# Attention tail split in two and the gate kept in another buffer, in a fused attention and channel-mix layer

## The reference

```python
x = x + LN(attention(LN(x)))      # 16 heads of 64, rope over the whole width, banded softmax
x = x + LN(channel_mix(LN(x)))

# attention: blocks of 512 queries see their own block and the one before, inside a band
q, k, v = h @ Wq.T + bq, h @ Wk.T + bk, h @ Wv.T + bv       # q, k then rope
scores = einsum('qd,kd->qk', q, k) / 8;  band = (j >= i) & (j <= i + 512)
out = softmax(where(band, scores, min)) @ v;  return out @ Wo.T + bo

# channel mix, x_prev is x shifted by one token
xr, xk = mu_r*x + (1-mu_r)*x_prev, mu_k*x + (1-mu_k)*x_prev
r = sigmoid(xr @ W_r.T)
return r * (square(relu(xk @ W_k.T)) @ W_v.T)
```

## Time and profile before

| | |
|---|---|
| Median of 2 runs | 6762.48 us (6732.92 and 6792.04) |
| The profiled execution | 6755.53 us, of which the span of the slowest core (core 3) is 6754.0 us |
| Spans of the 8 cores | 6704.8 to 6754.0 us |
| Busy: PE, DVE, ACT, POOL | 3167.8, 3086.4, 1531.8, 874.3 us |
| Mean busy share of the 16 DMA engines by queue | 9.1%, 6.1%, 2.9% and less |
| Chain that ended last, by engine | PE 34%, DVE 33%, ACT 9%, issue 7%, DMA 7%, SPq 5% |

### The profile page before, as it was taken

How to read it: one execution, slowest core, us unless ns; L and a number is a source line. 1 busy time by engine, 2 the same in 40 slices (tenths; PEclk the granted TensorE clock), 3 DMA queues, 4 the chain that set the end, 5 groups by cost and what they waited for, 6 DMA issues and landing times.

```text
span 6754.0 us, 51815 instructions; the slowest of 8 cores (6704.8 to 6754.0 us)
## 1 busy us (share of the span) xinstructions
PE 3167.8 (47%) x11840; PEld 1243.5 (18%) x11840; DVE 3086.4 (46%) x4185; ACT 1531.8 (23%) x2881; POOL 874.3 (13%) x644
## 2 busy tenths in 40 slices
PE   0435526355254545545454364553645365363654
PEld 0112212122121212212121121221211122121221
DVE  2454344444454445344455444544445543444434
ACT  0111403214021220412203041130411114132141
POOL 0011211111111110211101011120111101111021
PEclk9857566575667657566575666656667575665756
DMA  6313020120201212012120301203012120211201
GB/s 198 95 38 87 4 98 24 38 87 4 97 25 59 66 38 87 1 59 66 34 91 19 94 13 50 75 19 94 13 50 75 38 87 1 93 32 38 87 0 56
DMA packets 251407, 376.76 MB, mean 56 GB/s; under 512 B 149730, under 2 KB 149730, under 8 KB 251108
## 3 DMA queue, kind: packets, MB, share of 16 engines
q1 hardware_dynamic: 185060, 163.72, 9.1%
q0 software_dynamic: 33792, 134.22, 6.1%
q10 hardware_dynamic: 32256, 75.51, 2.9%
HBM read 264.33 MB, written 75.50 MB: 50 GB/s over the span
## 4 chain that ended last, share of the span: by engine, by line
PE 34%; DVE 33%; ACT 9%; issue 7%; DMA 7%; SPq 5%; POOL 3%; DVEq 1%; ACTq 1%; POOLq 0%
DVE ybuf L473 13%; PE pb L461 8%; ACT pk L434 7%; PE pb L427 5%; PE pb L325 5%; DVE scr L249 5%; SPq L173 4%; PE pb L593 4%; PE pb L376 4%; PE pb L614 3%; DVE ssum L246 3%; DMA xsl<-x 2%; PE pb L476 2%; POOL ybuf L530 2%; DVE qx L560 1%
## 5 line engine op out<-in xcount | busy, mean ns | idle before, releaser
L473 DVE RECIPROCAL ybuf<-pb 1x512 bf16<-1x512 f32 x256 | 858.1, 3352 | 1315.5 <-PE pb L461 1315.5
L434 ACT ACTIVATE pk<-pb,neg 128x512 bf16<-128x512 f32 (+3 forms) x1792 | 945.2, 527 | 1091.5 <-PE pb L427 863.0
L593 PE MATMUL pb<-WS,qx 128*128 128x512 bf16 x1024 | 264.5, 426 | 1195.1 <-DVE qx L571 1194.2
L427 PE MATMUL pb<-qx,krot 64*128 64x512 bf16 (+3 forms) x1792 | 673.7, 431 | 293.9 <-ACT pk L434 237.9
L325 PE MATMUL pb<-hfm,Wwq 128*128 128x512 bf16 x1024 | 267.0, 420 | 971.0 <-DMA hfm<-hstage 971.0
L476 PE MATMUL pb<-ybuf,onesb 1*64 1x512 bf16 x256 | 153.8, 601 | 924.1 <-DVE ybuf L473 924.1
L461 PE MATMUL pb<-pk,vext 128*65 128x128 bf16 (+3 forms) x2368 | 525.8, 406 | 2.0
L445 POOL TENSOR_TENSOR pk<-pk,tri0s 128x512 bf16<-128x512 bf16 x192 | 220.8, 1150 | 2223.5 <-ACT pk L434 2223.5
L449 POOL TENSOR_TENSOR pk<-pk,tri4s 128x512 bf16<-128x512 bf16 x256 | 293.9, 1148 | 1003.4 <-ACT pk L434 1003.4
L593 PEld LDWEIGHTS pb<-WS,qx 128*128 128x128 bf16 x1024 | 108.1, 107 | 1348.2 <-issue 1263.6
L461 PEld LDWEIGHTS pb<-pk,vext 128*65 128x65 bf16 x2368 | 311.7, 172 | 173.8 <-issue 78.7
(11 more groups left out here) (89 smaller groups left out, 3490.8 us busy)
## 6 DMA issues: line engine op xcount, KB each, us to landing
xsl<-x SPq DMA_DIRECT2D x128, 512.0 KB, 5.6
WS<-wo_bf POOLq DMA_DIRECT2D x16, 2048.0 KB, 13.3
WS<-wr_bf POOLq DMA_DIRECT2D x16, 2048.0 KB, 19.4
WS<-wk_bf POOLq DMA_DIRECT2D x16, 2048.0 KB, 10.0
WS<-wv_bf POOLq DMA_DIRECT2D x16, 2048.0 KB, 10.0
out<-ybuf ACTq DMA_DIRECT2D x64, 512.0 KB, 2.7
hstage<-htm ACTq DMA_DIRECT2D x64, 256.0 KB, 2.6
cosb<-cosd SPq DMA_DIRECT2D x64, 256.0 KB, 3.8
```

Of the source, the lines that this page charges most:

```text
L427: qlo=qlo, qhi=qhi: e.matmul(pb[bk][:, qlo:qhi], ksrc[po:po + 64, BS * md + 128 * tc:BS * md + 128 * (tc + 1)], qx[po:po + 64, BS * md + q ...
L434: texp = cop("scalar", lambda e, bk=bk, c=c, qlo=qlo, qhi=qhi, pku=pku: e.activation(out=pku[:, BS * c + qlo:BS * c + qhi], in_=pb[bk][:, ...
L473: t_rc = cop("vector", lambda e, rb=recipb[uslot], ub=ub: e.reciprocal(rb, pb[ub][64:65, :]), waits=[t_av, buf.get(("recip", uslot)), prev ...
L593: ins = e.matmul(pb[bk][:, :], qx[:, BS * ci + 128 * tj:BS * ci + 128 * (tj + 1)], WS[1][:, D * ci + BS * hh:D * ci + BS * (hh + 1)], star ...
```

## The change

It has three parts.

1. `plan_tail` is cut into `plan_av` (AV matmuls, copy to `usb`, reciprocal) and `plan_norm` (the spreading matmul L476 and the product L480). The loop now has 18 steps and calls, for i: scores of head i, `plan_av` of head i - 1, `plan_norm` of head i - 2. Work per head is the same; its order on PE and DVE is another.
2. The AV bank is 3 + h % 3, one of three, and no longer 4 + h % 2.
3. r goes to `qx` and not to `htm`. A token group's r overwrites the 128 columns of each chunk of `qx` which that group's gate matmuls have read, so both halves' matmuls are issued first, and both sigmoids wait for both. The sigmoid's output, and the two inputs of the multiply after `v2mm`, become patterns of 4 runs of 128 elements. `buf["htm"]` is now the store of the second layer norm's result, and `buf["qx"]` the last multiply.

```diff
-        def plan_tail(h):
-            md, po = h // 2, 64 * (h % 2)
+        tails = {}
+
+        def plan_av(h):
             exp_toks, gm, pku = hstate.pop(h)
-            ub = 4 + h % 2
+            ub = 3 + h % 3
...
+            tails[h] = (ub, uslot, t_uc, t_rc)
+            return t_av
+
+        def plan_norm(h):
+            md, po = h // 2, 64 * (h % 2)
+            ub, uslot, t_uc, t_rc = tails.pop(h)
             bb = 6 + h % 2
...
-        for i in range(NH + 1):
+        for i in range(NH + 2):
             if i < NH:
                 plan_scores(head_order[i])
-            if i > 0:
-                t_av_last = plan_tail(head_order[i - 1])
+            if 1 <= i <= NH:
+                t_av_last = plan_av(head_order[i - 1])
+            if i >= 2:
+                plan_norm(head_order[i - 2])
...
         for tj in range(4):
+            tms = []
             for hh in range(2):
...
-                tmm = cop("tensor", rmm, waits=[bank_free[bk], t_wr] + t_mixr, tok=True)
-                wr_users.append(tmm)
-                trs = cop("scalar", lambda e, bk=bk, tj=tj, hh=hh: e.activation(
-                    out=htm[:, D * tj + BS * hh:D * tj + BS * (hh + 1)], in_=pb[bk][:, :],
-                    func=AF.Sigmoid), waits=[tmm, t_h2w[-1], buf.get(("r", tj, hh))], tok=True)
+                tms.append(cop("tensor", rmm, waits=[bank_free[bk], t_wr] + t_mixr, tok=True))
+            wr_users += tms
+            for hh in range(2):
+                bk = 2 + hh
+                rap = bass.AP(qx[:, :].tensor, 2048 * hh + 128 * tj,
+                              [[4096, 128], [512, 4], [1, 128]])
+                trs = cop("scalar", lambda e, bk=bk, rap=rap: e.activation(
+                    out=rap, in_=pb[bk][:, :], func=AF.Sigmoid),
+                    waits=tms + [buf.get(("r", tj, hh))], tok=True)
                 t_rsg.append(trs)
                 bank_free[bk] = trs
...
-                tfe = cop("vector", lambda e, sl=sl, hh=hh, bk=bk, tj=tj: e.tensor_mul(
-                    aof[sl][:, BS * hh:BS * (hh + 1)], pb[bk][:, :],
-                    htm[:, D * tj + BS * hh:D * tj + BS * (hh + 1)]),
+                rap = bass.AP(qx[:, :].tensor, 2048 * hh + 128 * tj,
+                              [[4096, 128], [512, 4], [1, 128]])
+                pin = bass.AP(pb[bk][:, :].tensor, 0, [[BS, 128], [128, 4], [1, 128]])
+                tfe = cop("vector", lambda e, sl=sl, hh=hh, pin=pin, rap=rap: e.tensor_mul(
+                    aof[sl][:, BS * hh:BS * (hh + 1)], pin, rap),
                     waits=[tmm, buf.get(("aof", sl))] + t_rsg, tok=True)
...
-        buf["htm"] = t_fe_all[-1]
+        buf["htm"] = t_h2w[-1]
         buf["hfm"] = h2l_tok
-        buf["qx"] = wr_users[-1]
+        buf["qx"] = t_fe_all[-1]
```

More of the change, by code:

```diff
@@ L486, in plan_tail @@
             t_attn_evac.append(t_ae)
-            return t_av
         t_av_last = None
-        for i in range(NH + 1):
+        for i in range(NH + 2):
             if i < NH:
                 plan_scores(head_order[i])
-            if i > 0:
-                t_av_last = plan_tail(head_order[i - 1])
+            if 1 <= i <= NH:
+                t_av_last = plan_av(head_order[i - 1])
+            if i >= 2:
+                plan_norm(head_order[i - 2])
         kv_cons[0] = kv_cons[1] = t_av_last
```

## The result

| | before | after |
|---|---|---|
| Median | 6787.66 us (10 runs, 6732.92 to 6840.09) | 6114.75 us (11 runs, 6066.94 to 6162.39) |
| Ratio to before | | 0.9004, 95% interval 0.8972 to 0.9037 |
| Profiled execution, span of its slowest core | 6754.0 us (core 3) | 6115.6 us (core 5) |
| Spans of all cores | 6704.8 to 6754.0 | 6047.9 to 6115.6 |

The change makes the kernel 10% faster. The forecast was 6024 us, with a range of 5860 to 6100; the median lies 15 us above the range. The direction, the place and the mechanism of the gain were as forecast. Two terms of the sum were mis-sized: attention gained 59 us less, and the gate lost 24 us more.

What follows compares the result with a forecast made beforehand. PE was taken to be bound by its 924.1 us wait for the reciprocal ahead of the spreading matmul. From 6755.5 us, attention gives 802 (664 and 138) and the gate costs 70: 6024 us, range 5860 to 6100.

Steps and rivals of the forecast that it cites:

- the ring of n > 0: Attention, 12 iterations: PE's repeating cycle per head falls from 10.60 to 6.84 us, 664 us less with the tail.
- DVE at n = 0: Attention, 4 iterations: DVE becomes the bound, 4.23 us a head, 5.6 at six bank reuses; 138 us less.
- some 20 for the last two heads: Sign: PE's idle time before the spreading matmul, released by the reciprocal, falls from 924 us to some 20.
- the subtraction of 0.26: Attention, n > 0: AV holds PE for 2.42 - 0.26 = 2.16 us, 0.26 being a reader's lag after the last matmul.
- The tail: End of attention, n > 0: last two reciprocals 4.23 us apart, then 5.10 to the output matmul; 9.3 together.
- the reuse after two heads costs nothing at n > 0: Attention: six AVs wait for a bank until 6.65 us after the AV before, 0.19 short of 6.84.
- the clock in the gate: Gate: the first group runs 8 matmuls at half clock in 3.41 us, then 8 at full clock in 1.73.
- The 59 us without a fall: Gate: 19.8 us where it is 16.10 now, +3.7 an iteration, 16 times, if the clock never falls.
- the fall after the first pause: Gate: after the 2.3 us pause the clock falls at evens, adding 11 us for +70 in all; 81 if always.
- the rival: Attention: the clock rises for single or all heads, n > 0 ring 6.0 us, total 5870; chance 0.22.
- the rival of half clock throughout: Gate and k matmuls: three pauses keep PE at 0.50, 386 us more, total 6400; chance 0.06.
- the slower rival: Attention: reciprocal and exp disturb each other, exps at 1.3 us instead of 0.66, total 6850; exps slowed 0.07, slower than before 0.02.

Runs made afterwards that it cites:

- the experiment with one wait less: Parts 1 and 2 with the AV bank numbered by head position, the spreading matmul also waiting for the previous head's product; ratio to the kernel before 0.8838.
- The two-bank kernel: Part 1 alone on the kernel before, the AV bank staying 4 + h % 2; median 6159.34 us.
- The preload experiment: The changed kernel plus one small unread sigmoid on ACT ahead of the gate, so the table load is done early; ratio to the kernel before 0.8966.
- the kernel with four score banks: The one-wait-less kernel with scores going round four banks and all spreading matmuls in bank 7; median 5843.18 us, ratio to the kernel before 0.8603.
- part 3 alone: Only part 3, the gate change, put on the kernel before; ratio to the kernel before 1.0107.

## Why the prediction was right, and where it failed

**The steps that failed** are terms of the sum: the gaps in the ring of n > 0 (6.84 us, measured 7.07) and on DVE at n = 0 (4.23 and 5.6, measured 4.45 and 5.88), and the clock in the gate, which rose later than the prediction had it and fell more often. The mechanism of each part held.

**What bounds the kernel, and the mechanism of part 1: right.** PE's wait for the reciprocal fell to 85.4 us where I had put some 20 for the last two heads. They do make most of it, 78 us on core 5, but at more than I had put: the last head's L483 waits 3.9 us and the one before 0.8 to 1.6, sixteen times. The other 7 us lie ahead of inner heads at n = 0.

**n > 0: right in kind, 0.22 us short in size.** My ring was 4.14 + 2.16 + 0.54 = 6.84, the measured one 4.27 + 2.24 + 0.56 = 7.07. Half of the difference, 0.11, is a cost of the new order that I had not counted: AV needs its own wait instruction for DVE, shown by the experiment with one wait less. Of AV's 2.16 the subtraction of 0.26 failed: I took the lag of a reader of another stage for this one, and PE's own change to L483 costs 0.08 more than that. 0.22 us in 14 intervals and 12 iterations make 37 us. The tail is 5.35 us from the last reciprocal to the output matmul and not 5.10, as the product of the head before stands in between:

```profile
1111.72 3.35 DVE L474 RECIPROCAL ybuf<-pb 1x512 bf16<-1x512 f32 x1 [0.17 <-DVE ax L487]
...
1116.24 0.68 DVE L487 TENSOR_TENSOR ax<-urt,pb 64x512 bf16<-64x512 bf16 x1 [0.24 <-DVE ax L487]
1117.07 3.57 PE L518 MATMUL pb<-WS,ax 128*128 128x512 bf16 x8 [1.25 <-DVE ax L487]
```

**n = 0: right that DVE becomes the bound and that six AVs pay for their bank; gaps too small.** I took 0.1 us for each gap on DVE, which none of my rows showed. They are 0.24 behind a reciprocal and 0.17 behind a product, so 4.45 and not 4.23, and 5.88 and not 5.6. From the first reciprocal to the first output matmul that is 79.9 us against my 76.0, 16 us over four iterations. With the 42 of n > 0 (108.6 against 105.1 us) this is 58 of the 59 us that attention missed.

**That the reuse after two heads costs nothing at n > 0: right,** with 6.65 us now 6.94 (2.42 + 3.35 + 0.24 + 0.68 + 0.25), still under 7.06. The two-bank kernel shows it for every head but the last, which I had left out; with three banks that one is covered.

**The gate: the pauses right, the clock wrong twice.** 2.3, 1.0 and 1.0 us are as forecast, and so is that nothing hides them. First, I let the clock rise 3.41 us after the first matmul, by the one row at 1347.3. The next row says otherwise: a mean of 0.98 over the 12.5 us behind it leaves some 0.5 us at half clock, so the rise was at about 1348.0, 4.1 us after the first matmul. In iteration 2 of the changed kernel it was 5.5, and the first 16 matmuls took 6.1 us, not 5.14. In the kernel before a late rise was mostly hidden, because the wait for the table load and the sigmoid held PE up anyway: on core 5 a gate took 16.1 us where the clock rose within 4.7 us, and 16.7 where it rose at 5.95. Part 3 takes this cover away. The second group started 8.23 us after the first in the mean, not 7.42, and that is 13 us over 16 gates. Second, I put the fall after the first pause at evens, from two iterations of another stage with a pause of 2.06 us. It fell in 15 of 16 on core 3, at 1.7 us each, 25 us in all. Two looks at another stage with a shorter pause were no sound basis, and more of them would not have helped: behind the 16 pauses of 2.06 to 2.43 us at that place the clock fell 6 times on core 3 before the change. The 59 us without a fall, 13 and 25, less 3.5 because the gates before took 16.3 us in the mean and not 16.10, make 93.5 of the 93.8 measured. In both kernels with part 3 the clock fell in the gates where it had risen late; why it rises late in one gate and early in another was not tried. The preload experiment shows that the fall needs the long first pause.

**The rivals.** The clock did not rise for all heads. The row for iteration 2 of core 3 (it answers to the first of the earlier trace rows) is

```profile
1010.40:1110.70 100.30, 83.37 (x288) 33.12 (x287) 57.16 (x28) 66.50 (x124) 32.18 (x28) 0.50 0.00 1
```

PE is busy 83% of the time where it was 56%, and in the row of the kernel with four score banks 87%, still at 0.50. For single heads it did rise, as the rival allowed. Between the last two reciprocals of some iterations with n > 0 the clock went above 0.50, here to 1.00 in iteration 7 of core 3:

```profile
2944.33 2.31 PE L462 MATMUL pb<-pk,vext 128*65 128x128 bf16 x11
...
2947.26 1.54 PE L462 MATMUL pb<-pk,vext 128*65 128x128 bf16 x11
```

```profile
2948.00:2951.20 3.20, 1.17 (x8) 0.49 (x5) 2.79 (x2) 0.08 (x1) 0.00 (x0) 1.00 0.00 0
```

There are no scores behind the last head's, so two AVs follow each other with only L483 between, and the second takes 1.54 us in place of 2.31. The clock went up there in 15 of 128 attention stages (16 iterations, 8 cores), and in 71 of 128 in the kernel with one wait less. It gains nothing, because DVE sets that last interval at 4.45 us. In the kernel with four score banks it went up instead in the second head, in 14 of 128, behind an AV and four scores without a pause. The Trainium skill says in "TensorE: Matmul & The Clock Gate", Part 1, that sustained activity releases the throttle. The trace agrees where PE worked without a pause, and over the heads with gaps it shows 0.50, so 0.22 for the rival was too much. In the gate, where PE works without a gap, the clock rises too. The gate's clock came back after the second group; the k matmuls kept their 246.4 us, so the rival of half clock throughout falls. Exps kept 527 ns and the copy 578 beside the reciprocal, which disposes of the slower rival. This agrees with the Trainium skill, "PSUM — Partial Sum Buffer", Specifications, by which ScalarE and VectorE access PSUM side by side at full bandwidth short of a bank collision.

**The sum and the range.** On the undisturbed cores the two mis-sized terms are +59 and +24. Between the slowest cores of the two profiled executions the time fell by 638 us, some 93 less than the forecast 732: 58 in attention, 16 in the gate and 37 in the projections and v, where the slowest core after the change ran at 0.81 for six iterations, less 17 elsewhere. That the median came to lie outside the range is in part an accident of the base: the median of the kernel before was 32 us above the 6755.5 that the forecast starts from, and the measured ratio of 0.9004 on that base would be 6083, inside the range. The terms were wrong all the same. The range's upper end of 6100 was built from my bounds on named costs, 81 at most for the gate where 94 were measured. It had nothing for many small gaps that each add 0.1 us to a ring of 7 that turns 168 times, nor for a clock that differs from run to run. Two products in the gate's working are slips that change little: 48 matmuls at 13.98 / 64 are 10.48 us and not 10.37, and the rival at half clock adds 376 us and not 386.

## What to carry to other kernels

Where an in-order engine waits in every turn of a ring for a long instruction of another, put the instruction that needs the result one turn later. Then count the whole new ring, hop by hop, with the gaps of the same instruction pairs and one more for each wait that another wait used to cover: here errors of about 0.1 us a hop made 58 us. A bank or buffer that rotates over positions in time should be numbered by position, not by the object's name. A condition put on another instruction because it is met there anyway has to be looked at in the last turn too, where nothing covers it. Where two halves of a pair share one wait, double the banks, and load an activation table before the stall that exposes it: the pause costs more than its length when the clock falls behind it.

## What the runs showed of the hardware

A semaphore wait on PE that is already met took 0.11 us of a ring. On DVE 0.24 us lie between a one-partition reciprocal and the product that follows it, 0.17 between a product and a reciprocal. PE's clock stayed at 0.50 over 87 us of attention with PE busy 87% and short gaps between its matmuls, and in the changed kernel went above it between the last two reciprocals in 15 of 128 stages. In the gate it rose 2.6 to 6.0 us after the first matmul, over the 8 cores of the kernels before and after; behind a pause of 2.3 us it fell to 0.50 in 105 of 128 gates (94 of 128 with part 3 alone), behind pauses of 1.0 us in none of the 128 gates with the table loaded ahead. Pairs of cores were granted 0.81 for stretches of one to six iterations, in either kernel.
